# Softmax of a window attention by sixteen biased exponentials per quad, with the mask written into PSUM by VectorE

## The reference

```
def local_attention(q, k, v):            # q, k: normalised per head and rotated
    bk2, bv2 = (look(bk), look(bv))      # each window's keys: the window before and its own, 64
    mask = (it < jb) | (it > jb + w) | (jb == -1)
    sim = jnp.einsum('bhwie,bhwje->bhwij', bq, bk2) * QK_SCALE
    sim = jnp.where(mask, -jnp.finfo(sim.dtype).max, sim)
    attn = jax.nn.softmax(sim, -1)
    out = jnp.einsum('bhwij,bhwje->bhwie', attn, bv2)
```

## Time and profile before

| | |
|---|---|
| median of 3 runs | 3166.56 us (3165.83 to 3168.74) |
| profiled execution | 3168.24 us, of which the span from first to last instruction 3166.5 |
| granted TensorE clock, mean | 0.99 |
| PE busy | 3005.7 us, 95% |
| DVE busy | 2880.3 us, 91% |
| ACT busy | 2272.7 us, 72% |
| POOL busy | 1807.9 us, 57% |
| a plain step | 61.34 us |
| a step with the retention | about 72 us |

### The profile page before, as it was taken

How to read it: one execution, slowest core, us unless ns; L and a number is a source line. 1 busy time by engine, 2 the same in 40 slices (tenths; PEclk the granted TensorE clock), 3 DMA queues, 4 the chain that set the end, 5 groups by cost and what they waited for, 6 DMA issues and landing times.

```text
span 3166.5 us, 93664 instructions
## 1 busy us (share of the span) xinstructions
PE 3005.7 (95%) x37896; PEld 1857.5 (59%) x37896; DVE 2880.3 (91%) x2671; ACT 2272.7 (72%) x3707; POOL 1807.9 (57%) x823
## 2 busy tenths in 40 slices
PE   8699999999999999999999999999999999999996
PEld 4356555665665566565566656556656555665653
DVE  5599999999999999999999999999999999999995
ACT  4467777777777777776667777777777777777774
POOL 8556565555656555555445565555656565555652
PEclk9799999999999999999999999999999999999998
DMA  9544544543544544454344354454445445445542
GB/s 317 169 110 116 144 115 107 145 122 98 156 117 101 144 117 117 118 154 113 84 133 106 91 152 117 107 133 124 112 121 141 112 122 133 112 118 134 125 112 59
DMA packets 254405, 398.04 MB, mean 126 GB/s; under 512 B 51148, under 2 KB 84872, under 8 KB 254280
## 3 DMA queue, kind: packets, MB, share of 16 engines
q1 hardware_dynamic: 254280, 396.41, 47.8%
HBM read 64.64 MB, written 19.92 MB: 27 GB/s over the span
## 4 chain that ended last, share of the span: by engine, by line
PE 40%; DVE 23%; ACT 19%; issue 10%; SPq 1%; POOL 1%; DMA 1%; DVEq 0%; ACTq 0%; POOLq 0%
PE ps L848 6%; PE ps L806 5%; PE ps L866 5%; PE ps L882 5%; PE ps L827 5%; PE ps L787 4%; ACT f_ab L1094 4%; DVE f_mx L1362 4%; DVE f_p L1365 3%; ACT f_u L1093 3%; DVE f_p L1377 3%; ACT ps L1105 3%; PE ps L789 3%; PE ps L788 3%; ACT f_p L1111 3%
## 5 line engine op out<-in xcount | busy, mean ns | idle before, releaser
L1291 POOL TENSOR_TENSOR f_w<-f_w,f_ab 128x1024 f32<-128x1024 f32 x192 | 549.2, 2861 | 526.9 <-DVE f_w L1342 526.9
L1296 POOL TENSOR_TENSOR f_ab<-f_w,f_rn 128x1024 f32<-128x1024 f32 x192 | 594.1, 3094 | 390.9 <-DVE f_rn L1352 380.9
L1287 POOL TENSOR_TENSOR f_u<-f_u 128x512 f32<-128x512 f32 x384 | 589.1, 1549 | 365.3 <-ACT f_u L1093 359.8
L1094 ACT ACTIVATE f_ab<-ps,f_pa 128x512 f32<-128x512 f32 x768 | 542.1, 706 | 1.2
L1093 ACT ACTIVATE f_u<-ps 128x512 f32<-128x512 f32 x768 | 467.1, 608 | 99.3 <-PE ps L789 93.6
L1342 DVE TENSOR_TENSOR f_w<-f_ab,f_tan 128x1024 f32<-128x1024 f32 x384 | 500.4, 1343 | 4.1 <-POOL f_ab L1296 2.3
L848 PEld LDWEIGHTS ps<-f_tb,f_v 128*64 128x64 f32 x6144 | 396.0, 137 | 102.1 <-issue 78.5
L848 PE MATMUL ps<-f_tb,f_v 128*64 128x160 f32 (+1 forms) x6144 | 442.2, 297 | 11.9 <-DMA f_tb<-f_pt 10.7
L1105 ACT ACTIVATE ps<-ps 128x512 f32<-128x512 f32 x384 | 204.7, 574 | 340.7 <-PE ps L806 340.2
L787 PE MATMUL ps<-f_xh,f_wh 128*128 128x512 f32 x768 | 380.7, 496 | 54.8 <-ACT f_ab L1094 44.5
L806 PE MATMUL ps<-f_u,f_ones 128*128 128x512 f32 x768 | 370.2, 604 | 6.9 <-POOL f_u L1287 4.1
(11 more groups left out here) (165 smaller groups left out, 4822.9 us busy)
## 6 DMA issues: line engine op xcount, KB each, us to landing
f_kb<-f_ab SPq DMA_DIRECT2D x384, 256.0 KB, 3.6
f_qb<-f_ab SPq DMA_DIRECT2D x384, 256.0 KB, 3.6
f_tb<-f_pt SPq DMA_DIRECT2D x1344, 64.0 KB
f_wh<-split_w SPq DMA_DIRECT2D x48, 384.0 KB, 4.4
f_wl<-split_w SPq DMA_DIRECT2D x48, 384.0 KB, 4.2
a_w_raw<-wqkv SPq DMA_DIRECT2D x24, 384.0 KB, 4.6
split_w<-a_w_hi SPq DMA_DIRECT2D x24, 384.0 KB, 4.6
split_w<-a_w_lo SPq DMA_DIRECT2D x24, 384.0 KB, 5.5
```

The source lines that it names most:

```text
L1094: nc.scalar.activation(ab[:, g % 2, i, :], bank("qk", g, i), ACT.Identity, scale=pa[:, g, i:i + 1]).then_inc(qk_read.sem, 1)
L1287: nc.gpsimd.tensor_tensor(u[:, 2 * i + 1, :], u[:, 2 * i, :], u[:, 2 * i + 1, :], ALU.add).then_inc(sq_sum[i].sem, 1)
L1291: nc.gpsimd.tensor_tensor(w[:, 0:2, :], w[:, 0:2, :], ab[:, k % 2, 0:2, :], ALU.add).then_inc(q_sum.sem, 1)
L1296: nc.gpsimd.tensor_tensor(ab[:, k % 2, 0:2, :], w[:, 0:2, :], rn[:, 0:1, :].broadcast_to([128, 2, N]), ALU.mult).then_inc(rope_q.sem, 1)
```

## The change

Each quad's softmax is done differently, and the mask gets into the score banks in another way.

- DVE writes the mask: a new `mask_scores(g)` copies the bf16 mask, read twice, into both score banks (1024 columns) once the exponentials of quad g - 1 have read them. All 64 products of `scores(g)` now add to it with start=False, and wait for `m_ready`. PE's two mask products, the identity `identb` and `mask_scores` on PE are gone. In step 0 two plain products with start=True write both banks once, ahead of everything, and `norms(g)` of later quads waits for DVE to have read the norm banks.
- DVE `less_maximum(g)` is now the reduction alone, with its sign turned.
- ACT `exponentials(g)` reads the scores from PSUM by sixteen activations of 64 columns; each has the negated maximum of its row as a per-partition bias, writes its row of `p` (two runs of 32), and leaves the row's sum in `rs` (`accum_out`). It waits for the maximum and for the transpose of the quad before, which frees `p`.
- DVE `sums(g)` is now the reciprocal alone.
- DVE's order changes: turn(1) and add_keys(1) come ahead of sums(-1); turn(2) and add_keys(2) ahead of sums(0); the mask of the next quad is written right before turn_weights(0) and turn_weights(1), right after turn_weights(-1), and right before turn_weights(2); evacuate_out comes ahead of sums(1); second_residual ahead of sums(2). ACT's order and PE's are the same but for PE's mask products.

```
-        s_max, s_sub, p_exp = per_quad("s_max"), per_quad("s_sub", ahead=1), per_quad("p_exp")
-        p_sum, p_inv, p_norm = per_quad("p_sum"), per_quad("p_inv"), per_quad("p_norm")
+        m_ready = per_quad("m_ready")
+        s_max, p_exp = per_quad("s_max"), per_quad("p_exp", ahead=1)
+        p_inv, p_norm = per_quad("p_inv"), per_quad("p_norm")
...
+                srow, rows_of = ps[:, SS[0]:SS[1] + 1, :].rearrange("p a (n k) -> p (a n) k", k=2 * WIN), pb.rearrange("p b n k -> p n b k")
...
                         def norms(g):
 
+                            if not prev and g:
+
+                                pe.wait_ge(gain.sem, now.count(gain, g - 1))
...
-                        def mask_scores(g):
-
-                            pe.wait_ge(s_sub.sem, now.count(s_sub, g - 1))
-                            nc.tensor.matmul(ps[:, SS[0], :], identb[:, :], mask[:, 128:640], start=True, stop=False, skip_group_check=True)
-
                         def scores(g):
                             pe.wait_ge(q_dma.sem, now.count(q_dma, g))
                             pe.wait_ge(k_dma.sem, now.count(k_dma, g))
-                            nc.tensor.matmul(ps[:, SS[1], :], identb[:, :], mask[:, 128:640], start=True, stop=False, skip_group_check=True)
+
+                            pe.wait_ge(m_ready.sem, now.count(m_ready, g))
+                            pe.sem_inc(scores_begun, 1)
...
                                 pe.wait_ge(masked, N_MASKED)
+                                for i in range(2):
+
+                                    nc.tensor.matmul(ps[:, SS[i], :], ones[:, :], tan2[:, 0, :], start=True, stop=True).then_inc(banks_begun, 1)
...
                         def exponentials(g):
-                            act.wait_ge(s_sub.sem, now.count(s_sub, g))
-                            nc.scalar.activation(p[:, :], p[:, :], ACT.Exp).then_inc(p_exp.sem, 1)
+                            act.wait_ge(s_max.sem, now.count(s_max, g))
+                            act.wait_ge(p_tr.sem, now.count(p_tr, g - 1))
+
+                            for n in range(16):
+                                last = nc.scalar.activation(rows_of[:, n], srow[:, n].rearrange("p (b k) -> p b k", b=2), ACT.Exp,
+                                                            bias=mx[:, n:n + 1], accum_out=rs[:, n:n + 1])
+                            last.then_inc(p_exp.sem, 1)
...
                         def less_maximum(g):
 
-                            srow = ps[:, 5:7, :].rearrange("p a (n k) -> p (a n) k", k=2 * WIN)
                             dve.wait_ge(s_ready.sem, now.count(s_ready, g))
-                            nc.vector.tensor_reduce(mx[:, :], srow, AX.X, ALU.max).then_inc(s_max.sem, 1)
-                            dve.wait_ge(s_max.sem, now.count(s_max, g))
-                            dve.wait_ge(p_tr.sem, now.count(p_tr, g - 1))
-                            nc.vector.tensor_tensor(rows_of, srow.rearrange("p n (b k) -> p n b k", b=2),
-                                                    mx[:, :].unsqueeze(2).unsqueeze(3).broadcast_to([128, 16, 2, WIN]), ALU.subtract).then_inc(s_sub.sem, 1)
+                            nc.vector.tensor_reduce(mx[:, :], srow, AX.X, ALU.max, negate=True).then_inc(s_max.sem, 1)
+
+                        def mask_scores(g):
+                            dve.wait_ge(p_exp.sem, now.count(p_exp, g - 1))
+                            if not prev and g == 0:
+                                dve.wait_ge(banks_begun, 2)
+                            nc.vector.tensor_copy(ps[:, SS[0]:SS[1] + 1, :], mask[:, 128:640].unsqueeze(1).broadcast_to([128, 2, N])).then_inc(m_ready.sem, 1)
 
                         def sums(g):
 
                             dve.wait_ge(p_exp.sem, now.count(p_exp, g))
-                            nc.vector.tensor_reduce(rs[:, :], rows_of, AX.XY, ALU.add).then_inc(p_sum.sem, 1)
-                            dve.wait_ge(p_sum.sem, now.count(p_sum, g))
                             nc.vector.reciprocal(rs[:, :], rs[:, :]).then_inc(p_inv.sem, 1)
...
                         if prev:
                             less_maximum(-1)
+                        if cur:
+                            turn(1)
+                            add_keys(1)
+                        if prev:
                             sums(-1)
-                        if cur:
-                            turn(1)
-                        if prev:
                             turn_weights(-1)
                         if cur:
-                            add_keys(1)
+                            mask_scores(0)
                             normalise_keys(1)
                             less_maximum(0)
-                            sums(0)
-                            turn_weights(0)
-                        if prev:
-                            residual()
-                        if cur:
                             turn(2)
                             add_keys(2)
-                        if prev:
+                            sums(0)
+                            mask_scores(1)
+                            turn_weights(0)
+                        if prev:
+                            residual()
                             centred()
```

More of the change, by code:

```diff
@@ L491, in build_hybrid @@
                     *((128, c) for c in range(-64, 33, 32)), *((512, c) for c in range(-640, -255, 128))]
-        ACT_USES = [(1, -1), (3, -5), (3, -4), (3, -3), *((4, c) for c in range(-3, 2)), *((8, c) for c in range(-7, 1)),
+        ACT_USES = [(1, -1), (3, -5), (3, -4), (3, -3), *((4, c) for c in range(-4, 2)), *((8, c) for c in range(-7, 1)),
                     *((16, c) for c in range(-15, 1)), (32, 32), *((128, c) for c in range(-96, 1, 32))]
@@ L532, in stage_ffn @@
                 consts, zeroed = sem("f_consts", scope), sem("f_zeroed", scope)
+                banks_begun = sem("f_banks_begun", scope)
                 masked, xs_first = sem("f_masked", scope), sem("f_xs_first", scope)
@@ L535, in stage_ffn @@
                 split_first = sem("f_split_first", scope)
-                N_CONST, N_MASKED = 6 * 16, 3
+                N_CONST, N_MASKED = 6 * 16, 2
                 block = scope.enter_context(nc.Block())
+                srow, rows_of = ps[:, SS[0]:SS[1] + 1, :].rearrange("p a (n k) -> p (a n) k", k=2 * WIN), pb.rearrange("p b n k -> p n b k")
                 def bank_of(order, *which):
@@ L1055, in step @@
                             values(0)
-                            mask_scores(2)
                         if prev:
@@ L1332, in bank @@
                             return bank_of(order, *which)
-                        f, rows_of = ps[:, FB, :], pb.rearrange("p b n k -> p n b k")
+                        f = ps[:, FB, :]
                         def turn(k):
@@ L1508, in step @@
                             add_keys(3)
+                            mask_scores(2)
                             turn_weights(1)
@@ L1516, in step @@
                             sums(2)
+                            mask_scores(3)
                             turn_weights(2)
@@ L1526, in step @@
                             less_maximum(-1)
-                            sums(-1)
                         if cur:
                             turn(1)
+                            add_keys(1)
                         if prev:
+                            sums(-1)
                             turn_weights(-1)
                         if cur:
-                            add_keys(1)
+                            mask_scores(0)
                             normalise_keys(1)
                             less_maximum(0)
+                            turn(2)
+                            add_keys(2)
                             sums(0)
+                            mask_scores(1)
                             turn_weights(0)
@@ L1551, in step @@
                             turn(3)
+                            evacuate_out()
                             sums(1)
-                            evacuate_out()
+                            mask_scores(2)
                             turn_weights(1)
@@ L1563, in step @@
                             normalise_keys(3)
-                            sums(2)
                         if prev:
@@ L1571, in step @@
                         if cur:
+                            sums(2)
+                            mask_scores(3)
                             turn_weights(2)
@@ L1580, in _ @@
                     nc.vector.tensor_copy(mask[:, :].rearrange("p (a n) -> p a n", a=2), hid[:, 0:2, 0:384]).then_inc(masked, 1)
-                    nc.vector.tensor_copy(identb[:, :], fc[:, 0:128]).then_inc(masked, 1)
                     nc.vector.tensor_copy(ones[:, :], fc[:, 128:256]).then_inc(masked, 1)
+                    dve.wait_ge(masked, N_MASKED)
                     steps_of(dve, step)
```

13 lines of the change are left out of this document (2 added, 11 removed).

## The result

The changed kernel takes 4105.3 us (4103.3 to 4109.6), the kernel before 3167.2 us (3165.8 to 3168.7): a ratio of 1.296 (1.294 to 1.299), 938 us more where 486 were forecast, and above the upper end of the range. The profiled execution took 4109.6 us, 1.8 outside its span of 4107.8. In the first round of experiments one run of the kernel before (3380 us) and one of e1_order (3959 us) were disturbed, with a lower granted clock than their fellows, and are left out.

The account below looks back on a forecast made before the run. PE (95%) and DVE (91%) were nearly full; ACT, 72%, waited on them. ACT's 61.6 us of work plus 10.3 of waits gave 71.9 us steps: 441 + 40 + 5 = 486 us more, said as 3650 us, range 3400 to 3860.

Parts of the forecast that it names:

- The price of an exponential with its sum: On ACT, each 64-column exponential with accumulated sum takes 0.30 us, so 4.8 us a quad instead of 0.96.
- ACT's work per step: ACT's busy time in a plain step rises from 46.2 to 61.6 us, before any wait.
- the mask copy: DVE's copy of the bf16 mask into two PSUM banks, 1024 columns, taken at 1.2 us, with 0.7 kept as alternative.
- Rivals 1 and 2: On ACT: 1, the sum is free, 3350 to 3480 us, chance 0.2; 2, pipe empties before sum, 3950 and above, 0.12.
- rival 3: ACT's idle time takes the added work and PE sets the step: faster, 3093 us, chance 0.05.
- rival 4: DVE's mask copy runs at the SBUF cast's pace, 0.7 us: 24 us less, inside the forecast, no separate chance.
- New waits that I cost at nothing: PE's scores waiting for the mask copy, and DVE's weights and next mask behind its wait for the exponentials: 0 us.
- the wait of shifted(): ACT's wait before shifted(), behind DVE's chain after exponentials(0): 2.8 us a step instead of 1.97.
- The last sentence of the prediction: Should PE's longer pauses lower its granted clock of 1.00, waits behind PE and the time grow; no size given.
- less the same share, I take +8 each: Five middle steps with retention: ACT's work 65.3 us, 21 us of waits less a share, +8 us each, 40 together.
- Before inverse_norms(1) ... Gone: ACT's wait before inverse_norms(1), about 1.1 us a step, is covered by the longer EXP(-1) and disappears.
- 2.74 + 2.77: ACT's waits behind PE that stay: 2.74 us before inverse_norms(0) and 2.77 before inverse_norms(3), a step.

Follow-up runs that it names:

- e1_order: Changed kernel with turn(2) and add_keys(2) put back behind residual() in the plain steps: 3829 us in a single run, 3863.3 us when timed again.
- e8_one_quad: Kernel before, with the sixteen biased exponentials and accumulated sums for quad 3 alone, mask and order as before: 3325.4 us, ratio 1.051.
- e4_order_fill: Changed kernel with turn(2) and add_keys(2) back behind residual() and filler products in three of PE's pauses: 3686.7 us, ratio 1.165.

## Why the prediction was wrong

Forecast 3650 us in the range 3400 to 3860, measured 4105.

**What held.** The price of an exponential with its sum, the term in which most of the doubt was placed: 0.289 us against 0.30, 4.63 us a quad against 4.8. ACT's work per step, 61.1 against 61.6. DVE, 52.8 against 53.1, and the mask copy at 1.205 us (192 copies, 231.4 us) against 1.2, at the pace of the PSUM subtraction and not at that of the cast in SBUF. shifted() without the moved turn, 2.6 us against 2.8. Rivals 1 and 2 fell with the row of the accumulator; rival 3 with e8_one_quad; rival 4 with the copy. The 4105 us lie where rival 2 was placed, at 3950 and above, but not by its mechanism, which wanted 0.40 us or more an exponential. The section of the Trainium skill that the prediction cites against small tiles, in "VectorE: DVE Perf Modes", speaks of operations with a source in SBUF. Rows 7 and 8 and the sixteen exponentials read PSUM, so they neither agree with that rule nor speak against it, and nothing in the sum rested on it.

**Where it failed first: "New waits that I cost at nothing", and the wait of shifted().** The sum for that wait took DVE's steps between exponentials(0) and the residual as reciprocal, copy, multiplication, transpose, residual. It looked at where the diff puts the mask copy and passed over the other lines of the same hunk, which put turn(2) and add_keys(2) ahead of sums(0). Two things follow that the trace of before could have told: L1342 of turn(2) needs a buffer that POOL's L1296 of quad 1 releases, and POOL's order puts the squares of quad 2, hence ACT's evacuation of quad 2, ahead of that. And the 3.5 us of the two themselves were in no term of the sum. 7.25 us instead of 2.8, 242 us in the whole (213 with the clock held up).

**Then: the clock.** The last sentence of the prediction named it and no number was put to it, nor was it a rival. The working took PE to be idle 14 us a step and left its rows at the prices of a granted clock of 1.00. In the trace of the changed kernel four of PE's pauses, of 2.20 to 4.90 us, are followed by rows at 1.2 GHz or partly so, and PE is busy 65.35 us a step instead of the 57.7 forecast. Part of this lies on what ACT waits for: norms(1), with 3.16 us in place of 1.88, and values(-3). ACT's waits before evacuate_out and before the gates, 3.2 us a step and forecast at nothing, are gone in e4_order_fill. 177 us with the order mended, 206 without.

**Third, and small: "less the same share, I take +8 each".** This is the term for the five steps with the retention. ACT's work in them was forecast at 65.3 us, and 64.8 were measured; with 21 us of waits that makes 86.3 against 71.9, +14, and the cut to 8 was not worked out. In e4_order_fill the four full ones take 88.4 to 89.1 us, 70 us more together than before, where four times 8 are 32. With the shorter ones on either side they take 91 us more, where the forecast has 50; that is the 37 us that are left, within a few. The clock is part of it, as the fillers are not in these steps and the granted clock in them is 0.92. No run isolates the two.

**Errors that cancel.** "Before inverse_norms(1) ... Gone" is wrong too: that wait is 1.99 us in the changed kernel. The evacuations ahead of it on ACT moved back as far as the longer EXP(-1), and PE with them. With clock and order mended the norms' waits are 6.3 us a step against 2.74 + 2.77 = 5.5, and the shorter exponential, the 2.6 us of shifted() and the wait for the maximum, 0.6 us where 0.86 were forecast, make up for it. That the plain step comes out at 71.87 us is in part luck.

**The range.** Its bounds were built from the price of one instruction, 0.20 to 0.36 us, and 2 us a step for the waits. The instruction came out within 4%. The waits were off by 10.5 us a step. The width stood on the wrong term. The sum of the bound has a slip as well: 0.36 us an exponential gives 3650 + 180 = 3830 and not 3770, and with the 90 for the waits 3920, still below 4105.

## What to carry to other kernels

Read each line of a hunk that reorders an engine's queue as an edit of its own: for every step moved ahead, ask which semaphore it waits for and what now stands behind that wait, on this engine and on the one that waits for it. When new work on one engine makes TensorE's pauses longer, price TensorE's rows at both clocks: here a kernel with 38 useless products more a step was 5% faster. And don't count an engine's idle share as room for work: here nine tenths of one quad's 3.67 us landed on the time although ACT was idle 15 of 61 us, because what ACT waits for is made by PE and DVE from what ACT gave them.

## What the runs showed of the hardware

- An activation with an accumulated sum is two instructions. With 64 columns the second, a read of 128x1, starts some 0.2 us after the first and costs 0.093 us: the pairs follow each other in 0.289 us, and exponentials without a sum in 0.196.
- A VectorE copy of 1024 bf16 columns from SBUF into PSUM in fp32 takes 1.205 us, about the 1.225 of an fp32 subtraction out of PSUM.
- Pauses of TensorE of 3.4 to 4.9 us were followed by rows at the lower clock. Behind a pause of 2.2 us the norms took 3.16 us in the changed kernel and 1.98 in the kernel with order and fillers, so a pause of that length goes either way. In the latter, with its mean clock at 0.98, the hidden products run at full speed (5.77 us) behind a pause of 1.12.
- VectorE's multiplications of two SBUF operands and GpSimd's additions, run together, took 4.28 and 3.51 us in place of 2.36 and 2.51 apart.
